# Two-layer cross-attention on one core: the normalised context turned on VectorE and carried to its place by 16 small transfers a group

## What is computed

```
x [8, 56, 256], context [8, 1500, 256];  16 heads of 128, layers 1 and 2:
h = layer_norm(x);  q = h @ wq + bq;  k = ctx @ wk + bk;  v = ctx @ wv + bv      (k and v with one bias row more)
weights = softmax(q k^T / sqrt(128));  x = x + (weights v) @ wo + bo
then x = x + gelu(layer_norm(x) @ w_fc1 + b_fc1) @ w_fc2 + b_fc2
```

## Time and profile before

| | us |
|---|---|
| median of 3 runs | 1295.76 (1294.04 to 1296.68) |
| the profiled execution, its own time | 1292.47 |
| its span, first to last instruction | 1290.7 |
| TensorE busy | 1253.4 |
| VectorE, ScalarE, GpSimd busy | 794.9, 804.4, 906.8 |

### The profile page before, as it was taken

The page is one execution under the profiler, slowest core; times in us unless marked ns, Lnnn a source line. Parts: engine busy times, 40 slices in busy tenths (PEclk is TensorE's granted clock), DMA queues, the critical chain, the costliest instruction groups (busy, mean ns, idle before and its releaser), DMA issues.

```text
span 1290.7 us, 26447 instructions
## 1 busy us (share of the span) xinstructions
PE 1253.4 (97%) x8100; PEld 1153.8 (89%) x8100; DVE 794.9 (62%) x1371; ACT 804.4 (62%) x1574; POOL 906.8 (70%) x750
## 2 busy tenths in 40 slices
PE   7999999999999999989989999999999999999898
PEld 6779999999999999978877999999999999999797
DVE  6755666666666666639675666666656565665564
ACT  4746666666656666666474666666666666667654
POOL 3746777777777686668573768686868687856782
PEclk8999999999999999999999999999999999999899
DMA  5401111111111111112251111111111111101121
GB/s 175 136 5 49 39 59 40 55 44 57 49 52 48 48 48 36 36 50 74 76 168 36 37 37 61 36 60 37 58 41 54 45 59 39 60 24 45 50 89 40
DMA packets 30414, 72.58 MB, mean 56 GB/s; under 512 B 3072, under 2 KB 4144, under 8 KB 30368
## 3 DMA queue, kind: packets, MB, share of 16 engines
q1 hardware_dynamic: 30368, 72.01, 17.9%
HBM read 71.52 MB, written 0.48 MB: 56 GB/s over the span
## 4 chain that ended last, share of the span: by engine, by line
PE 89%; DVE 4%; ACT 3%; issue 2%; DMA 1%; POOL 1%; DVEq 0%; SPq 0%; ACTq 0%; POOLq 0%
PE psum L648 35%; PE psum L669 13%; PE psum L671 12%; PE psum L670 12%; PE psum L616 5%; PE psum L702 4%; PE psum L680 2%; DMA w_raw<-weights 1%; PE psum L637 1%; PE psum L662 1%; PE psum L655 1%; PE psum L693 1%; POOL pt L490 1%; DVE qh L1146 1%; DVE g_prod L1137 1%
## 5 line engine op out<-in xcount | busy, mean ns | idle before, releaser
L490 POOL TENSOR_TENSOR pt<-slots,pt 125x512 fp32r<-125x512 f32 (+1 forms) x384 | 445.8, 1165 | 218.0 <-ACT slots L929 185.7
L648 PE MATMUL psum<-qs,ctx 128*125 128x384 f32 (+1 forms) x2304 | 540.7, 371 | 1.3 <-ACT slots L960 0.8
L648 PEld LDWEIGHTS psum<-qs,ctx 128*125 128x125 f32 x2304 | 394.6, 186 | 46.7 <-ACT slots L960 8.2
L669 PE MATMUL psum<-ctx,pt 125*128 125x258 f32 x1344 | 385.7, 287 | 5.3 <-ACT on L935 4.4
L670 PE MATMUL psum<-ctx,pt 125*128 125x256 f32 x1344 | 379.3, 282 | 0.0
L671 PE MATMUL psum<-ctx,pt 125*128 125x258 f32 x1344 | 379.3, 282 | 0.0
L1201 DVE TENSOR_TENSOR t_max<-psum,t_max 125x512 f32<-125x512 f32 (+1 forms) x320 | 199.3, 623 | 260.6 <-PE psum L648 260.3
L928 ACT ACTIVATE pt<-slots 125x512 fp32r<-125x512 f32 (+1 forms) x384 | 221.2, 576 | 192.8 <-DVE slots L1189 179.0
L960 ACT ACTIVATE slots<-psum 125x512 f32<-125x512 f32 (+1 forms) x384 | 207.2, 540 | 140.5 <-DVE t_max L1201 132.8
L669 PEld LDWEIGHTS psum<-ctx,pt 125*128 125x128 f32 x1344 | 253.5, 189 | 22.6 <-ACT on L935 11.8
L670 PEld LDWEIGHTS psum<-ctx,pt 125*128 125x128 f32 x1344 | 254.1, 189 | 6.0
(11 more groups left out here) (89 smaller groups left out, 1076.0 us busy)
## 6 DMA issues: line engine op xcount, KB each, us to landing
nat_stage<-ctx_nat SPq DMA_DIRECT2D x64, 375.0 KB
tr_stage<-ctx_tr SPq DMA_DIRECT2D x64, 375.0 KB, 3.1
w_raw<-weights SPq DMA_DIRECT2D x72, 256.0 KB, 2.7
dk_all<-dk_rows SPq DMA_DIRECT2D x2, 768.0 KB, 6.3
dk_all<-dk_rows SPq DMA_DIRECT2D x2, 256.0 KB, 4.4
xres<-x_rows SPq DMA_DIRECT2D x4, 112.0 KB, 2.2
out_rows<-xres SPq DMA_DIRECT2D x4, 112.0 KB, 1.9
bo<-out_bias SPq DMA_DIRECT2D x1, 336.0 KB, 3.7
```

Source lines behind the costliest of these rows:

```text
L490: nc.gpsimd.tensor_tensor(split_weights(h, LO, c), slot(h, c), as_f32(split_weights(h, HI, c)), ALU.subtract).then_inc(pt_lo, 1)
L648: last = mm(scores(h, k), ctx_tr_chunk(half, a, c), qs[h][:, m, half, 0:R], start=(half, a, m) == terms[0], stop=(half, a, m) == terms[-1])
L669: mm(O_BANK[j][:, 0:D + 2], hi, ctx_nat_hi(c), start=(c == 0), stop=False, skip_group_check=True)
```

## The change

The context is no longer turned by TensorE, except that of the last half of each layer, which is turned as before behind the last weighted sums (`last_context`). For every other half, at c = 7 VectorE transposes all of `on` in one instruction into a new tile `turn`. That instruction turns each block of 32 x 32 within itself: inside a quarter of 32 partitions the numbers are turned, but the blocks stay in the quarter of partitions in which they lay. So 16 transfers follow, one for each pair of source quarter and goal quarter, each 32 partitions x 8 (or 6) runs x 32 numbers, that is 32 KB (24 KB) in runs of 128 bytes. ScalarE issues them from its own queue, four at the head of each of the steps c = 8 to 11, ahead of that step's exponentials. The first waits for `turned`; VectorE's next transposition waits for `moved`, the landing of all 16. Both `normalized` wait for the turn of the half before, since it reads `on`.

`qt` becomes tile by tile ([128, 56 tiles, 2, 128] in place of [128, 2, 8, 896]), so that a run goes to one place; the views of it follow. The output bias is loaded a layer at a time, which makes room. TensorE's waits for `OT_BANK` go with its transposes.

```diff
-        qt = sb("qt", [P, DC, B, FLAT], F32)
+        qt = sb("qt", [P, NT, DC, P], F32)
...
+        turn = sb("turn", [P, GT[0], D], F32)
...
@@ SyncE
+            def load_bias(m):
+                sp.wait_ge(xb_ready, INIT + m * RG)
+                sp.dma_start(bo[:], out_bias[m:m + 1, :].rearrange("a n -> (a n)").partition_broadcast(RGP)).then_inc(
+                    bo_in, 16)
...
@@ TensorE, batch_steps
-                            pe.wait_ge(ot_out, INIT + group * 2 - 4)
+                            pe.wait_ge(max_ready, INIT + group - 1)
                             max_transposes(1 - h)
...
-                        if c in (6, 8) and not first:
-                            if c == 6:
-                                pe.wait_ge(max_ready, INIT + group)
-                            group_transposes(b - 1, h, c // 2 - 3, OT_BANK)
...
@@ ScalarE
                     act.wait_ge(rden_ready, INIT + l * GROUPS + b * 2 + (h + 1))
+                    act.wait_ge(turned, INIT + l * (GROUPS - 1) + b * 2 + h)
...
+                def move_context(b, h, i):
+                    if i == 0:
+                        act.wait_ge(turned, INIT + l * (GROUPS - 1) + b * 2 + (h + 1))
+                    rows, dims = divmod(i, QUARTERS)
+                    source = turn[rows * QUARTER:(rows + 1) * QUARTER, 0:GT[h]].rearrange(
+                        "p j (c q r) -> p j c q r", c=DC, q=QUARTERS)[:, :, :, dims].rearrange("p j c r -> p (j c) r")
+                    goal = qt[dims * QUARTER:(dims + 1) * QUARTER, ds(b * TILES + h * GT[0], GT[h])].rearrange(
+                        "p n c (q r) -> p n c q r", q=QUARTERS)[:, :, :, rows].rearrange("p n c r -> p (n c) r")
+                    act.dma_start(goal, source).then_inc(moved, 16)
...
+                        if c >= NCT - MOVES // MOVES_STEP and not first and not (tail and h == 1):
+                            at = MOVES_STEP * (c - NCT) + MOVES
+                            for i in range(at, at + MOVES_STEP):
+                                move_context(b - 1, h, i)
...
-                        if c in (6, 8) and not first and not (tail and h == 1):
-                            transposed_context(b - 1, h, c // 2 - 3)
...
@@ VectorE
+                def turn_context(b, h):
+                    dve.wait_ge(on_act, INIT + l * (2 * GROUPS) + b * 4 + (2 * h + 2))
+                    dve.wait_ge(on_dve, INIT + l * (3 * B) + b * 3 + (2 + h))
+                    dve.wait_ge(moved, (l * (GROUPS - 1) + b * 2 + h) * (MOVES * 16))
+                    V.transpose(turn[:, 0:GT[h]], on[:, 0:GT[h]]).then_inc(turned, 1)
...
+                        if c == TURN_STEP and not first and not (tail and h):
+                            turn_context(b - 1, h)
```

More of the change, by code:

```diff
@@ L56 @@
 SPLIT_NEXT, SPLIT_SECOND = (12, 15), (0, 4)
+QUARTER, QUARTERS = 32, 4
+MOVES = QUARTERS * QUARTERS
+TURN_STEP, MOVES_STEP = 7, 4
 NAT_W = 2 * D + 2
@@ L106, in build @@
         col = sb("col", [P, N_COLS], F32)
-        bo = sb("bo", [RGP, 3, D], F32)
+        bo = sb("bo", [RGP, D], F32)
         lb = sb("lb", [P, NT], F32)
@@ L205, in build @@
         x_in = [sem(f"x_in{g}") for g in range(RG)]
-        tables_in, consts_in = sem("tables_in"), sem("consts_in")
+        tables_in, consts_in, bo_in = sem("tables_in"), sem("consts_in"), sem("bo_in")
         setup_step = sem("setup_step")
@@ L232, in build @@
         ot_mm, ot_out = sem("ot_mm"), sem("ot_out")
+        turned, moved = sem("turned"), sem("moved")
         pn_picked = sem("pn_picked")
@@ L239, in build @@
         settled = sem("settled")
-        N_TABLES, N_CONSTS = 2, 4
+        N_TABLES, N_CONSTS = 2, 3
         def settle(eng):
@@ L253, in build @@
                     dv_ready, gp_ready, gp_used, q_lo, first_qs_lo, lb_rows_ready, nat_hi, tr_hi, lb_ready, max_done,
-                    mt_reduced, max_ready, px_ready, sub_done, den_ready, rden_ready, pn_ready, on_dve, p80_lo,
+                    mt_reduced, max_ready, px_ready, sub_done, den_ready, rden_ready, pn_ready, on_dve, turned, p80_lo,
                     oth_lo, c_lo, xb_ready],
@@ L261, in start, with of_tiles @@
                 eng.sem_inc(counter, INIT)
-        qt_flat = qt[:].rearrange("p c b f -> p c (b f)")
+        qt_tiles = qt[:].rearrange("p n c r -> p c n r")
         def head_rows_of(h):
-            return qt[:].rearrange("p c b (t h e) -> p c (b t) h e", h=H, e=TQ)[:, :, :, ds(h, 1)].rearrange(
+            return qt[:].rearrange("p n c (h e) -> p c n h e", h=H, e=TQ)[:, :, :, ds(h, 1)].rearrange(
                 "p c n a e -> p c n (a e)")
+        def of_tiles(ap):
+            return ap.rearrange("p (n r) -> p n r", r=P)
         def by_tile(ap):
@@ L363, in _ @@
                 sp.dma_start(w_raw[u][:], weights[u]).then_inc(w_in[u], 16)
-            sp.dma_start(bo[:], out_bias.partition_broadcast(RGP)).then_inc(consts_in, 16)
             sp.dma_start(mask[:], mask_in).then_inc(consts_in, 16)
@@ L398, in batch_loads @@
                             load_tr(b + 1, tr + p, p)
+                load_bias(l)
                 batch_loads(0, True, False)
@@ L411, in _ @@
                         load_weight(l * JOBS + quad * 4 + (H + 4 + u), u, None)
+            load_bias(LAYERS)
             for u in range(4):
@@ L446, in split_q @@
             def split_q(b, h, half, n):
-                src = qt_flat[:, half, ds(b * FLAT + h * GT[0] * P, GT[h] * P)]
-                nc.gpsimd.tensor_copy(qs[h][:, HI, half], src).then_inc(qs_hi, 1)
+                src = qt_tiles[:, half, ds(b * TILES + h * GT[0], GT[h])]
+                nc.gpsimd.tensor_copy(of_tiles(qs[h][:, HI, half]), src).then_inc(qs_hi, 1)
                 pool.wait_ge(qs_hi, INIT + n + 1)
                 settle(pool)
-                nc.gpsimd.tensor_tensor(qs[h][:, LO, half], src, as_f32(qs[h][:, HI, half]),
+                nc.gpsimd.tensor_tensor(of_tiles(qs[h][:, LO, half]), src, of_tiles(as_f32(qs[h][:, HI, half])),
                                         ALU.subtract).then_inc(qs_lo, 1)
@@ L795, in group_contexts @@
                     last.then_inc(pv_mm, 1)
[L797 to L805, removed]
                 def batch_steps(b, first, tail):
@@ L845, in _ @@
                 last.then_inc(pn_picked, 1)
-                group_transposes(B - 1, 1, 0, OT_BANK)
-                group_transposes(B - 1, 1, 1, OT_BANK)
+                pe.wait_ge(on_act, INIT + (l + 1) * (2 * GROUPS))
+                pe.wait_ge(on_dve, INIT + (l + 1) * (3 * B))
+                context_transposes(0, 2, OT_BANK)
+                pe.wait_ge(ot_out, INIT + l * 2 + 1)
+                context_transposes(2, GT[1], OT_BANK)
                 heads, jobs = l * H, l * JOBS + H
@@ L920, in _ @@
                 for half in range(DC):
-                    go(qs[0][:, HI, half], qt_flat[:, half, 0:GT[0] * P], ACT.Copy).then_inc(first_qs_hi, 1)
+                    go(of_tiles(qs[0][:, HI, half]), qt_tiles[:, half, 0:GT[0]], ACT.Copy).then_inc(first_qs_hi, 1)
                 act.wait_ge(lb_ready, INIT + l + 1)
@@ L936, in normalized, with last_context @@
                            scale=rden[:, ds(b * TILES + (h * GT[0] + j), 1)]).then_inc(on_act, 1)
[L938 to L943, removed]
-                       ACT.Copy).then_inc(ot_out, 1)
+                def last_context(pair):
+                    j0, j1 = 2 * pair, min(2 * pair + 2, GT[1])
+                    act.wait_ge(ot_mm, INIT + l * 2 + pair + 1)
+                    go(qt_tiles[:, :, NT - (GT[1] - j0):NT - (GT[1] - j1)],
+                       OT_BANK[:, 0:DC * (j1 - j0) * P].rearrange("p (c n r) -> p c n r", c=DC, r=P),
+                       ACT.Copy).then_inc(ot_out, 1)
+                def move_context(b, h, i):
[7 more added lines that the diff above has]
+                    act.dma_start(goal, source).then_inc(moved, 16)
                 def batch_steps(b, first, tail):
@@ L980, in _ @@
                     weight_hi(l * JOBS + (H + u), u, l * 8 + 4)
-                transposed_context(B - 1, 1, 0)
-                transposed_context(B - 1, 1, 1)
-                act.wait_ge(ot_out, INIT + (l + 1) * (2 * GROUPS))
+                last_context(0)
+                last_context(1)
+                act.wait_ge(ot_out, INIT + (l + 1) * 2)
+                act.wait_ge(moved, (l + 1) * (GROUPS - 1) * MOVES * 16)
                 def context_hi(h, s, free):
@@ L1075, in add_bias @@
             def add_bias(m):
+                dve.wait_ge(bo_in, m * 16 + 16)
                 for g in range(RG):
-                    V.tensor_tensor(xres[:, g, :], xres[:, g, :], bo[:, ds(m, 1), :].rearrange(
-                        "p a d -> p (a d)"), ALU.add).then_inc(xb_ready, 1)
+                    V.tensor_tensor(xres[:, g, :], xres[:, g, :], bo[:], ALU.add).then_inc(xb_ready, 1)
             def nat_part_hi(n, p):
@@ L1177, in _ @@
                     dve.wait_ge(first_qs_hi, INIT + l * DC + half + 1)
```

(4 more changed lines are left out.)

## The result

The changed kernel takes **1352.58 us** (median of 4 runs, 1351.27 to 1353.71), beside 1294.9 (1291.01 to 1296.68) for the kernel before on the same chip: 1.0453 times as long [1.0436, 1.047]. It is slower by 57.7 us, on the side that I gave 0.43, and above my whole range.

What follows compares the result with a forecast made beforehand. TensorE was taken to bound the kernel. Transposes gone (-20.9 us), loop waits (+9.1) and longer layer tails (+6.2) gave -5.6 us, from a median of 1295.76 to 1290.2 us, range 1279 to 1330.

Steps and rivals of the forecast that it cites:

- the side that I gave 0.43: Whole kernel: chance of coming out slower, summed from three rivals at 0.31, 0.07 and 0.05.
- p: ScalarE's queue: distance from one transfer issue to the next, taken as 0.50 us, bounds 0.46 and 0.53.
- -20.9 + 9.1 + 6.2 = -5.6: Whole kernel, in us: TensorE's transposes gone, waits in the loop added, longer layer tails added, net gain.
- issue is the bound: Rival for ScalarE's loop steps: dear issues make copies late; 1303 us at 0.53 an issue, 1332 at 0.60; chance 0.31.
- 4p + 0.77: ScalarE's loop step with four issues: issuing resumes 0.25 us after the second exponential began; 2.77 us in the first half.
- The loop: Attention loop: TensorE waits for ScalarE's late copies, 0.65 us a batch over 14 batches, +9.1 us.
- The transposes: TensorE in the attention loop: 224 context transposes, 1.5 us a batch, 20.9 us gone over both layers.
- The turn: VectorE after step 7 of each half: block transposition taken as 1.2 and 0.95 us, twice that as upper bound.
- the rival of a double price: VectorE's turn takes double, adding 22 us in the loop, kernel at 1313 us; chance 0.07.
- The landings: Transfers land within the half batch of 31.5 us, hidden; the rival of late landings gave 1347 us, chance 0.05.
- The tails: End of each layer: ScalarE's issues delay GpSimd's last split and TensorE's last chunk, 3.1 us each, +6.2 us together.
- an estimate of 0.43 us an issue: ScalarE's queue, from the skill's 512 sequencer cycles at 1.2 GHz: the loop loses nothing, kernel at 1281 us.

Runs made afterwards that it cites:

- e2: The changed kernel with each transfer carrying only the first half of the dimensions, 128 runs in place of 256 and half the bytes: 1352.54 us.
- e7: The changed kernel with the transfers' goal a scratch tensor in DRAM in place of `qt`, same source, pattern and number: 1284.51 us.
- e5: The changed kernel with each partition's bytes as one run on both sides, same transfer sizes, to wrong places: 1320.77 us.
- e4: The changed kernel with the same 16 transfers a half issued from SP's queue between its loads, not ScalarE's: 1277.92 us.
- e1: The changed kernel without the 16 transfers a half and the waits for them, VectorE's turn kept: 1270.84 us.
- e3: The changed kernel with the same 16 transfers a half issued two a step over eight steps in place of four over four: 1277.81 us.
- e6: The changed kernel with the last of each step's four transfers left out, so three a step, twelve a half: 1282.34 us.
- e8: The changed kernel with two transfers a step from ScalarE in the loop and those in a layer's tail issued from SP: 1271.55 us.

## Why the prediction was wrong

**The step that failed is p**, the distance from one issue to the next. I put it at 0.50 us, between 0.46 and 0.53, and wrote that on this figure all turns. It is 0.72. With it the sum -20.9 + 9.1 + 6.2 = -5.6 became -21.0 + 60.5 + 17.8 = 57.3. All my rows were of loads from HBM, and I let them stand for transfers with SBUF on both sides. I kept a door open for an issue that grows with its runs; the price came, but that isn't its reason (e2). By e7 a goal in SBUF instead of DRAM is 0.28 us of the 0.615, by e5 0.08 hangs on the pattern, and by e4 ScalarE's queue adds next to nothing (0.615 for 0.608). So the rival "issue is the bound" is what happened, by its place (copies late in steps 8 to 11) and its wait, at a p beyond the 0.60 for which I gave 1332. Its 0.31 should have been more: no row bounded p from above, and I treated the nearest rows as if they did.

**The mechanism held.** ScalarE issues, its copy comes late, TensorE's scores wait for it. e1, e3, e6 and e8 take the excess away by removing, spreading or relocating the issues, e3 and e8 with every transfer still made.

**What ScalarE needs beside the issues** was mis-sized the other way. I took a step as 4p + 0.77, with nothing issued until the second exponential had begun; the rows have 4p + 0.21 (4p + 0.29 in e5). At my own p of 0.50 the loop would then not wait at all (4 x 0.5 + 0.21 = 2.2 against 2.485), and e7 shows that: loops of 456.2 and 456.7, as with no transfers, where I had forecast 9.1 us of waits. So break-even is at p = (2.485 - 0.21) / 4 = 0.57, or 0.55 with e5's 0.29. The two errors cover each other partly: at p = 0.72 my formula has a step of 3.66, the rows 3.10.

**The loop** thus gives 30.4 and 30.1 us of waits a layer (486.6 - 456.2, 486.6 - 456.5), 4.3 a batch, for which I had 0.65. From TensorE's step starts in the middle of layer 0, beside those of e1: in a first half four steps are 0.60 to 0.70 us too long, and with a rest of 0.10 in the next one that is 2.7. The first copy is late already: step 8's is there at 338.00 + 0.58 = 338.58, and TensorE could have used it at 335.49 + 2.48 = 337.97. In a second half two steps are 0.69 and 0.84 too long, and then comes step 24, which is long anyway; that is 1.6.

**The transposes:** 10.7 + 10.3 = 21.0 us in the loops by e1, predicted 20.9. **The turn:** 1.23 and 0.97, predicted 1.2 and 0.95; the rival of a double price falls. **The landings** were hidden, as said, and no turn waited for them: 6.6% of the engines for 116224 packets, where at the 0.122 us a packet of the earlier trace rows it would have been 66%.

**The tails** cost 8.7 and 9.1 us for my 3.1 each. Rows of the first one:

```profile
587.78 0.62 ACTq L961 DMA_DIRECT2D qt<-turn  x1
...
591.18 1.96 ACTq L961 DMA_DIRECT2D qt<-turn  x3
593.24 0.52 ACT L933 ACTIVATE pt<-slots 125x384 fp32r<-125x384 f32 x1 [1.81 <-issue]
...
595.98 0.52 ACT L933 ACTIVATE pt<-slots 125x384 fp32r<-125x384 f32 x1 [1.81 <-issue]
```

```profile
603.39 1.01 POOL L506 TENSOR_TENSOR pt<-slots,pt 125x384 fp32r<-125x384 f32 x1
```

```profile
600.89 0.58 PE L685 MATMUL psum<-ctx,pt 125*128 125x258 f32 x1 [1.39 <-POOL pt L506]
601.70 0.42 PE L685 MATMUL psum<-ctx,pt 125*128 125x258 f32 x1
602.35 0.42 PE L685 MATMUL psum<-ctx,pt 125*128 125x258 f32 x1
```

ScalarE's step is 2.74 us (595.98 - 593.24), for which I had 2.0: four of them, 3.0. Without a register instruction an issue follows another after (1.96 - 0.61) / 2 = 0.67 us, where I had 0.46; so this is the same error on p. The issues start 13.4 us after the loop's end (587.78 - 574.39), for which I had 562.8 - 550.71 = 12.1: 1.3 more. So GpSimd's last split starts 29.0 us after the loop's end, before 572.21 - 550.71 = 21.5: 7.5 of the 8.7, which is 3.1 + 3.0 + 1.3. The chain that I had drawn was right, its links too short. The remaining 1.2 us lie behind that split and go with TensorE's clock, which I hadn't thought of. Windows of that tail (columns as in the earlier trace rows, the clock third from the end):

```profile
592.00:600.00 8.00, 4.04 (x27) 3.41 (x27) 0.00 (x0) 3.15 (x7) 2.74 (x4) 1.00 0.30 47
600.00:607.00 7.00, 6.11 (x27) 5.87 (x27) 0.00 (x0) 2.36 (x6) 5.26 (x5) 0.51 0.17 42
```

TensorE had stood still 1.4 us in each of the steps before, about half of the stretch; then the granted clock is 0.51, the lower level, and three products take 602.35 - 601.70 = 0.65 us for 0.36. TensorE then works without a pause. GpSimd's last split is over at 603.39 + 1.01 = 604.40, but the nine products that need it start at 604.92 and take some 1.9 us, where before they started 0.05 after the split and took 1.2: together the 1.2. In the second tail the last split starts 30.0 us after the loop's end, for 21.5 before, which is 8.5 of the 9.1, since one of its issues took 1.05 us; the clock in its last weighted sums is 0.76, and what lies behind the split is 0.6 us longer. In e7, at the p that I had taken, the tails are 3.3 and 4.4 us longer than before, near my 3.1. In e8, where the tail's issues are on SP, they are 24.3 and 24.2.

The Trainium skill (DMA: Bandwidth & Descriptors, "Why a DMA increments its semaphore by 16 and not by 1") led to an estimate of 0.43 us an issue, at which nothing would be lost in the loop. Neither kind agrees: 0.615 from SBUF into SBUF, 0.336 into DRAM. Its advice to coalesce ("Rules for kernel authors") was the better guide, and e2 agrees: half the bytes cost as much. Here it is no overhead of the DMA engines but time of the queue that issues, and in the loop that mattered only above a threshold.

**Open:** what in a transfer from SBUF to SBUF takes the sequencer 0.28 us longer than one to DRAM. A goal in SBUF alone isn't it: the loads from DRAM in e4 take 0.29 us, though with other patterns. I tried neither the transfers' own pattern from DRAM to SBUF nor one with more partitions.

## What to carry to other kernels

An issue holds its engine's queue, and its price goes by the kind of transfer: before putting transfers on an engine that computes, find a row with the same kind of source and goal, and where there is none, let the upper bound stay open. Then compare by the step, not by the sum: here (issues a step) x p plus 0.2 to 0.3 us against the step of the engine that waits. Below that they were free in the loop (three a step, e6), above it nearly every step with issues paid, so the same 16 transfers cost 7 us spread out (e3), 1 us with the tails on an idle queue (e8), and 82 us in fours.

## What was unexpected

- An issue of these transfers from SBUF to SBUF takes 0.615 us on ScalarE and 0.608 on SP, 0.537 with one run a partition, and 0.336 when the goal is in DRAM. With 128 or 256 runs it is the same.
- ScalarE's sequencer goes on to the next transfer while exponentials and copy still run: issues at 337.37 and 338.09 beside exponentials at 337.15 and 337.58 and a copy at 338.00.
- 13.92 MB in 116224 packets of mostly 128 bytes fill 6.6 to 7.0% of 16 engines, that is 0.066 x 1351.1 x 16 / 116224 = 0.012 us a packet.
- Waits of 1.4 us in a row on TensorE were followed by its lower clock (0.51), so that a delay elsewhere was paid again in the products behind it.
